# A perceiver block on one core: the first token tile takes its products in another order, the first loads are shared 1 to 3 between two queues, and GpSimd makes three remainders

## The reference

```
q = (layernorm(x) @ q_proj_w.T)            # 512 x 4096, 32 heads of 128
k, v = ctx @ k_proj_w.T, ctx @ v_proj_w.T  # 8 heads of 128, 256 context rows a batch
q, k = rmsnorm(q) * q_norm_w, rmsnorm(k) * k_norm_w
x = x + softmax(q k^T / sqrt(128) + mask) v @ o_proj_w.T
x = x + causal self-attention with rotary positions (layernorm(x))
x = x + stream mixing with 50 Sinkhorn iterations (layernorm(x))
```

## Time and profile before

| | |
|---|---|
| median of 3 runs | 1132.21 us |
| profiled execution | 1133.6 us, span 1131.7 us |
| TensorE busy | 1064.2 us, 94% of the span |
| VectorE, ScalarE, GpSimd busy | 828.8, 476.6 and 159.1 us |
| granted TensorE clock over the span | 0.98 of full speed |
| bytes moved | 111.26 MB, mean 98 GB/s |

### The profile page before, as it was taken

One profiled execution on the slowest core, in us unless ns is written; L12 is line 12 of the kernel. 1 busy time (PEld: TensorE's weight loads), 2 busy tenths in 40 slices (PEclk: granted clock), 3 DMA queues, 4 the chain that ended last, 5 costly groups with the idle time before them and its releaser, 6 DMA issues.

```text
span 1131.7 us, 17533 instructions
## 1 busy us (share of the span) xinstructions
PE 1064.2 (94%) x6308; PEld 894.0 (79%) x6308; DVE 828.8 (73%) x1886; ACT 476.6 (42%) x1012; POOL 159.1 (14%) x162
## 2 busy tenths in 40 slices
PE   4999999999999999999999999999999999898736
PEld 3888888788888887888888887888888788787525
DVE  6787668676767868766678876675547798837998
ACT  4553434444444456454544454441224334321315
POOL 0000000322332232332333220000001000000000
PEclk9999999999999999999999999999999999989778
DMA  9785775244443333344445313899835313000001
GB/s 234 154 202 126 160 162 137 67 109 98 107 107 74 75 70 75 77 106 107 93 95 109 69 25 72 174 217 242 176 75 107 62 30 48 2 14 1 1 1 74
DMA packets 184540, 111.26 MB, mean 98 GB/s; under 512 B 108040, under 2 KB 174344, under 8 KB 184480
## 3 DMA queue, kind: packets, MB, share of 16 engines
q1 hardware_dynamic: 182224, 109.37, 44.9%
q10 hardware_dynamic: 2256, 1.11, 0.5%
HBM read 90.98 MB, written 18.94 MB: 97 GB/s over the span
## 4 chain that ended last, share of the span: by engine, by line
PE 83%; DVE 13%; ACT 2%; issue 1%; DMA 1%; ACTq 0%; POOL 0%; DVEq 0%
PE ps L606 29%; PE ps L513 15%; PE ps L573 13%; PE ps L939 9%; PE ps L499 4%; PE ps L617 4%; PE ps L634 4%; DVE wt L1501 1%; DVE small L2051 1%; DVE small L2055 1%; DVE small L2043 1%; DVE small L2047 1%; PE ps L717 1%; DVE small L2039 1%; DVE small L2035 1%
## 5 line engine op out<-in xcount | busy, mean ns | idle before, releaser
L606 PE MATMUL ps<-wt,act 128*128 128x512 f32 x1536 | 381.0, 394 | 0.0
L606 PEld LDWEIGHTS ps<-wt,act 128*128 128x128 f32 x1536 | 278.1, 188 | 51.8 <-issue 0.4
L513 PE MATMUL ps<-wt,act 128*128 128x512 f32 x768 | 177.3, 392 | 3.7 <-DVE wt L1501 3.7
L513 PEld LDWEIGHTS ps<-wt,act 128*128 128x128 f32 x768 | 144.7, 189 | 34.2 <-DVE act L1485 4.1
L573 PE MATMUL ps<-act,wt 128*128 128x512 f32 x672 | 153.7, 390 | 0.0
L573 PEld LDWEIGHTS ps<-act,wt 128*128 128x128 f32 x672 | 125.8, 188 | 26.0
L1056 ACT ACTIVATE wt<-raw 128x512 fp32r<-128x512 f32 x192 | 106.3, 625 | 92.4 <-PE ps L513 52.4
L1501 DVE TENSOR_TENSOR wt<-raw,wt 128x512 fp32r<-128x512 f32 x192 | 120.0, 682 | 25.9 <-ACT wt L1056 25.9
L939 PE MATMUL ps<-wt,act 128*128 128x512 f32 x480 | 124.5, 409 | 0.6 <-DVE wt L1501 0.6
L1493 DVE STREAM_TRANSPOSE raw<-raw 128x1024 f32<-128x1024 f32 x92 | 107.9, 1217 | 21.9 <-DMA raw<-in_L_xattn_o_proj_w 21.9
L2202 POOL TENSOR_TENSOR small<-small 128x4 f32<-128x4 f32 (+2 forms) x64 | 68.8, 1077 | 286.2 <-DVE small L1515 214.0
(11 more groups left out here) (161 smaller groups left out, 1205.2 us busy)
## 6 DMA issues: line engine op xcount, KB each, us to landing
xr<-in_ctx SPq DMA_DIRECT2D x64, 256.0 KB, 4.9
raw<-in_L_xattn_o_proj_w SPq DMA_DIRECT2D x32, 512.0 KB, 14.3
raw<-in_L_xattn_q_proj_w SPq DMA_DIRECT2D x28, 512.0 KB, 9.4
xr<-q_rows SPq DMA_DIRECT2D x16, 512.0 KB, 4.2
ot_hi<-spare SPq DMA_DIRECT2D x64, 128.0 KB, 2.0
act<-ot_hi SPq DMA_DIRECT2D x32, 256.0 KB, 9.3
q_rows<-G SPq DMA_DIRECT2D x28, 256.0 KB, 2.8
raw<-in_L_xattn_k_proj_w SPq DMA_DIRECT2D x8, 512.0 KB, 6.8
```

What stands on the lines that cost most here:

```text
L513: mm = pe.matmul(banks[t], lhs(p == 2, c, t), wt[:, n_slot, int(p == 1), c, :], start=(acc_from and q == 0), stop=(acc_to and q == 3 * NC ...
L606: mm = pe.matmul(bank, src[int(p == 2)][:, c, kt * P:(kt + 1) * P], wt[:, slot, int(p == 1), c, :], start=(q == 0), stop=(q == 3 * NC - 1))
```

## The change

There are four edits:

1. **Queues.** Of the four pieces of each half of unit 0, SP's queue issues one and ScalarE's three (two and two before).
2. **Order of products** in tile 0 of unit 0. First the products with rounded weights (p = 0 and p = 2) for chunks 0 to 7, then those with remainders (p = 1) for chunks 0 to 7. The waits follow: p = 0 waits for the rounded chunk (`w_hi`) and, every four chunks, for the rounded half of the activations (`hi_done`); p = 2 for the activations' remainder (`lo_done`); p = 1 for the weight's remainder (`w_lo`). The transposes of tile 1 come behind q = 7 in place of 11.
3. **GpSimd** makes the remainders of chunks 0, 1 and 2 of unit 0, the third behind the root and shift of tile 1. VectorE makes those of 3 to 7, and both halves of the activations' remainder of tile 0 directly behind the first two transposes.
4. **ScalarE** rounds weight chunk 0 between the two halves of the activations.

```diff
@@ sync
-            for dst, rows in first_unit(0)[0:2]:
+            for dst, rows in first_unit(0)[0:1]:
                 sp.dma_start(dst, rows).then_inc(first_half, 16)
             sp.dma_start(xr[:, 1, :], x_rows[:, 1, :]).then_inc(x_loaded[1], 16)
-            for dst, rows in first_unit(1)[0:2]:
+            for dst, rows in first_unit(1)[0:1]:
                 sp.dma_start(dst, rows).then_inc(raw_loaded[0], 16)
@@ tensor, products
-                        c, p = divmod(q, 3)
+                        c, p = order[q] if order and t == 0 else divmod(q, 3)
                         if arrived and p == 0:
                             arrived(t, c)
-                        if chunks and t == 0 and p == 0:
+                        if order and t == 0 and p == 2 and c % 4 == 0:
+                            pe.wait_ge(lo_done, c // 4 + 1)
+                        if chunks and t == 0 and p == int(bool(order)):
                             pe.wait_ge(w_lo, NC * n + c + 1)
@@ tensor, ln_ready
-                if c % 4 == 0:
+                if t == 0:
+                    pe.wait_ge(w_hi, c + 1)
+                    if c % 4 == 0:
+                        pe.wait_ge(hi_done, c // 4 + 1)
+                elif c % 4 == 0:
                     pe.wait_ge(lo_done, 2 * t + c // 4 + 1)
+
+            leading = [(c, p) for c in range(NC) for p in (0, 2)] + [(c, 1) for c in range(NC)]
...
-            query_unit(0, 0, lambda t: None, next_ln, chunks=True, arrived=ln_ready, at={1: 17, 2: 17})
+            query_unit(0, 0, lambda t: None, next_ln, chunks=True, arrived=ln_ready, at={0: 7, 1: 17, 2: 17},
+                       order=leading)
@@ scalar
-            for dst, rows in first_unit(0)[2:4]:
+            for dst, rows in first_unit(0)[1:4]:
                 sc.dma_start(dst, rows).then_inc(first_half, 16)
-            for dst, rows in first_unit(1)[2:4]:
+            for dst, rows in first_unit(1)[1:4]:
                 sc.dma_start(dst, rows).then_inc(raw_loaded[0], 16)
             normalise(0)
-            hi_ln(0, 0, T)
-            for c in range(4):
+            hi(0, 0, ln_dst(0, 0, 0), bank=T)
+            hi_w(0, 0, 0)
+            hi(1, 1, ln_dst(0, 0, 1), bank=T)
+            for c in range(1, 4):
                 hi_w(0, 0, c)
@@ vector
-            ln_lo_half(0, 0)
-            for c in range(4):
-                lo_unit(0, c)
+            ln_lo(0, 0, T)
             first_stats(1)
             turn_first(2)
             turn_first(3)
-            ln_lo_half(0, 1)
-            for c in range(4, NC):
+            v.wait_ge(w_lo, 3)
+            for c in range(3, 7):
                 lo_unit(0, c)
             ln_lo_half(1, 0)
+            lo_unit(0, 7)
+            ln_lo_half(1, 1)
             first_stats(2)
-            ln_lo_half(1, 1)
             first_stats(3)
@@ gpsimd
+            def lo_first(c):
+                pool.wait_ge(w_hi, c + 1)
+                pool.tensor_tensor(blocks16(wt_dst(0, 1, c)), raw_chunks(0, c), blocks16(wt_dst(0, 0, c)).bitcast(F32),
+                                   ALU.subtract).then_inc(w_lo, 1)
+
+            ln_root(0)
+            ln_move(0)
+            lo_first(0)
+            lo_first(1)
+            ln_root(1)
+            ln_move(1)
+            lo_first(2)
-            for k in range(NT):
+            for k in (2, 3):
                 ln_root(k)
                 ln_move(k)
```

More of the change, by code:

```diff
@@ L502, in products @@
             def products(n, n_slot, banks, lhs, before, acc_from=True, acc_to=True, between=None, chunks=False,
-                         arrived=None, at=None):
+                         arrived=None, at=None, order=None):
                 for t in range(NT):
@@ L529, in _, with query_unit @@
             pe.wait_ge(ident_ready, 16)
-            def query_unit(n, par, before=None, between=None, chunks=False, arrived=None, at=None):
+            def query_unit(n, par, before=None, between=None, chunks=False, arrived=None, at=None,
+                           order=None):
                 if not chunks:
@@ L539, in query_unit @@
                 products(n, par, acc, lhs_of(0), before or acc_ready, between=between, chunks=chunks,
-                         arrived=arrived, at=at)
+                         arrived=arrived, at=at, order=order)
             pe.wait_ge(ln_done, 1)
```

## The result

The changed kernel takes 1140.85 us (median of 4, 1139.96 to 1141.70) against 1132.74 (4 runs) for the kernel before: ratio 1.007, 95% interval 1.0055 to 1.0086. A later series on another chip (5 and 21 runs) gave 1.0085 (1.0072 to 1.0099), 1141.37 against 1131.72. It is slower by 8 to 10 us, as forecast. The profiled execution took 1140.15 us, its span 1138.0.

A forecast was written before the change was run, and what follows sets the result against it. TensorE, busy 94% of 1131.7 us, bounds the kernel, so tile 1's start decides: 28.0 + 7.0 = 35.0 against 25.2, 9.8 us later. 1133.6 + 9.8 = 1143.4, median 1.4 below: 1142.0; range 1133.0 to 1144.5.

The forecast's parts named there:

- The instant to look at: TensorE's start of the 24 products of tile 1 in a stretch without waits: 35.0 against 25.2, 9.8 us later.
- Nothing behind gives it back: After tile 1's start: unit 1 is in by 28.7 both times, unit 2 lands early, so all 9.8 us stay.
- Queue shares: DMA engines take one packet from each queue in turn, whatever its size; 0.029 us for 512 B, 0.075 1 KB, 0.21 4 KB.
- T1: Landing of the first half of unit 0's weights, when its transposes start: 17.8 in place of 11.7 us.
- T2: Landing of the second half of unit 0's weights: 28.0 in place of 18.0 us.
- the lower bound of 24.3: Earliest landing of the second weight half, if 1 KB packets cost nothing beside 512 B ones: 3.7 us less than 28.0.
- ScalarE's seven issues: Seven transfers in place of five; sixth waits until about 13 us; hidden behind T1, without that cover up to 4 us.
- Order, GpSimd, VectorE: New product order and moved remainders gain some 1.6 us at tile 1's transposes, swallowed ahead of T2: cost and gain nothing.
- The clock: TensorE slow after standing still some 3 us: from T2 to tile 1 6.45 to 7.9 us, 7.0 taken.
- A: Rival: queues share by bytes or landings don't hang on the queue; T1, T2 stay, 1131.4 to 1132.9; chance 0.14.
- B: Rival: ScalarE's queue catches up, T2 at 23 to 24.3, +5 to +6 us, 1137 to 1138; chance 0.18.
- C: Rival: landings stay, ScalarE's blocked issue delays the first product some 1.7 us; 0 to +1.5, 1132 to 1133.7; chance 0.06.

The follow-up runs named there:

- the run with small x packets: Changed kernel, shares 1 and 3, with x tiles 1 to 3 moved in 512 B packets in place of 4 KB; ratio 1.0006 to the kernel before.
- the run with shares back: Changed kernel with queue shares back at 2 and 2, new order of products and remainders kept; ratio 0.9995 to the kernel before.
- shares 3 and 1: Three pieces of each half on SP, one on ScalarE: in the changed kernel ratio 0.9992, in the kernel before 0.9997.
- the kept-busy run: Changed kernel with shares 2 and 2 and three extra unused products on TensorE; ratio 1.0001 to the kernel before.
- the run with shares 3 and 1 kept busy: Changed kernel with three pieces on SP, one on ScalarE, and three extra unused products on TensorE; ratio 0.9992 to the kernel before.

## Why the prediction was right

**The instant to look at.** Tile 1 was to start 9.8 us later; it started 10.6 and 8.4 later in two profiles. "Nothing behind gives it back" held up to 940 us, as far as one profile can be laid beside another. The forecast of 1142.0 is a ratio of 1.0087; measured were 1.0070 (up to 1.0086) and 1.0085, so it was right in kind and up to 2 us dear. The upper end of the range, 1144.5, is not its own sum: 28.7 + 7.9 - 25.2 = 11.4, which is 1143.6. Nothing rests on it.

**Queue shares.** One packet a turn was read from few rows. At 4 KB, 1 KB and 512 B it holds in the stretches of these runs from 8 us on, as long as both queues have work, and the run with small x packets shows it by itself. T1 was put at 17.8 and came at 16.6 and 14.9, before the 17 to 18 that were to show it; T2 was put at 28.0 and came at 27.5 and 25.6, the second outside 26 to 28.5. The terms were dear, by 0.5 to 3 us. Part of it is a step that was wrong: the turns were counted from 5 us, and from 5 to 8 us the queues do not take turns. In the changed kernel:

```profile
q1 hardware_dynamic: 184, 0.38, 65.3%
q10 hardware_dynamic: 501, 0.25, 48.5%
```

ScalarE's queue got 317 packets more than SP's, 20 an engine. Without 20 packets of unit 1 ahead of it, at 0.075, an estimate by the same sum has T1 at 16.3 and T2 at 26.5. Why the turns begin only then is not shown. The open price, 1 KB packets beside small ones, is settled: from 18 to 20 us 302 pairs fill 32 engine-us, 0.106 each, and 0.029 + 0.075 = 0.104 had been taken. They cost nothing less beside each other, so the lower bound of 24.3 falls.

**ScalarE's seven issues.** The sixth piece was to wait until about 13 and hide behind T1. The last issue ended at 11.99 (2.80 + 9.19), the activations were rounded in part before the first transposes ended, and product one waited for the rounded weight (18.52, T1 + 2.0). So it was hidden, as said.

**Order, GpSimd, VectorE.** Product one at T1 + 2.0 and the end of the statistics at +5.2 came as worked out. GpSimd's remainder of 128x512 took 1.27 us, next to the 1.2 by size; the third was done at 23.9, and VectorE's first remainder behind it began at 29.8. That all this is swallowed by T2 is shown by VectorE's idle of 5.76 us ahead of the third transposes. Without the late T2, in the run with shares back, the ratio shows no gain either (0.9984 to 1.0006); the six or seven slow products of that run fit this, and no run has them taken away.

**The clock.** 7.0 us had been taken from T2 to tile 1, between 6.45 and 7.9. It was 8.3 and 8.0: after the gap of 3.52 us not eight or nine but twelve or thirteen products ran at 0.43. This term was too small by 1.0 to 1.3, and T2 was too large by 0.5 and 2.4. That the start came out within 1.4 us of the forecast both times is in part the luck of two errors against each other.

**The rivals.** A, shares by bytes, falls by the run with small packets. The Trainium skill ("DMA: Bandwidth & Descriptors", Issuing engines are not separate DMA queues) has a second issuer save issue time alone. Here moving two of the eight pieces from one issuer to the other moved the landing of the last from 18.0 to 27.5, and moving two the other way to some 16, so the measurement goes against it. Of B, that ScalarE's queue catches up, the start is there (501 packets to 184 from 5 to 8 us) and the rest is not: 301 packets to 302 from 18 to 20 us, with T2 at 25.6 and 27.5 and not 23 to 24.3. C's blocked issue is there and decides nothing.

## What to carry to other kernels

In these runs, from 8 us on, the two queues share the DMA engines by packets, with packets of 512 B, 1 KB and 4 KB. So count packets, not bytes: a queue of short runs beside one of long rows gets a small part of the bandwidth (0.09 MB beside 0.58), and a piece moved to it comes later, though all the bytes are the same. What is wanted first should be in the queue that carries the large packets, ahead of them; or the large transfers should be held back or cut into small runs. Each of the three brought the landing forward here. A better order of work moved the start of tile 1 only where the landing it waits for came early (23.0 against 24.8 with shares 3 and 1); so look for the last wait of the stage first.

## What I had not expected of the hardware

- The granted clock in the view by stretches reads 1.00 for the first 18 us of the kernel before (for 15 to 17 see the earlier trace rows), while products there take 0.43 to 0.5; the products' own durations tell the speed at the start, the column does not. Later it does: 0.51 in the row of the kept-busy run, where products take 0.43.
- In a stretch in which TensorE is busy 94% (122 of 130 us), its clock fell to half for some 10 us in one profiled execution and for 3 in another, and the view reads 1.00 in the run with shares 3 and 1 kept busy. One profile against one profile can be 3.4 us off by that alone, more than most of the changes tried here bring over the kernel before.
- A queue alone moved 887 packets of 512 B in two microseconds; two queues together moved 1103.
- The landing of the same transfers differs by up to 1.9 us between executions of one kernel (27.5 and 25.6).
